# A distance-weighted attention in a twelve-part decoder kernel: one written order for all engines, with its grid computed inside the attention ahead of it

## The reference, cut to what matters

```python
scores = jnp.einsum('bhid,bhjd->bhij', qh, kh) / jnp.sqrt(jnp.float32(DH))
s_ = jnp.where(maskb, scores, -1e+32)
p = jax.nn.softmax(s_, axis=-1) * maskb.astype(scores.dtype)
cum = jnp.cumsum(p, axis=-1)
tot = jnp.sum(p, axis=-1, keepdims=True)
pos = jnp.abs(idx[None, :] - idx[:, None]).astype(scores.dtype)[None, None]
dist_scores = jnp.sqrt(jnp.clip((tot - cum) * pos, 0.0, None))
gamma = -jax.nn.softplus(gammas)[None]
diff = jnp.exp(jax.nn.sigmoid(pdiff))[:, None]
total_effect = jnp.clip(jnp.exp(dist_scores * gamma * diff), 1e-05, 100000.0)
scores = scores * total_effect
scores = jnp.where(maskb, scores, -1e+32)
scores = jax.nn.softmax(scores, axis=-1)
scores = scores.at[:, :, 0, :].set(0.0)
return jnp.einsum('bhij,bhjd->bhid', scores, vh)
```

## Time and profile before

| | us |
|---|---|
| median of 3 runs | 1520.55 (1520.49 to 1525.33) |
| the profiled execution | 1524.32 |
| its span | 1522.5 |
| DVE busy in it | 1058.7 (70%) |
| PE busy | 923.5 (61%) |
| ACT busy | 600.3 (39%) |
| POOL busy | 116.3 (8%) |

### The profile page before, as it was taken

How to read it: one execution, slowest core, us unless ns; L and a number is a source line. 1 busy time by engine, 2 the same in 40 slices (tenths; PEclk the granted TensorE clock), 3 DMA queues, 4 the chain that set the end, 5 groups by cost and what they waited for, 6 DMA issues and landing times. The chain is left out here.

```text
span 1522.5 us, 18302 instructions
## 1 busy us (share of the span) xinstructions
PE 923.5 (61%) x6195; PEld 610.9 (40%) x6195; DVE 1058.7 (70%) x2437; ACT 600.3 (39%) x1197; POOL 116.3 (8%) x249
## 2 busy tenths in 40 slices
PE   4844243445885204437979636999685405876877
PEld 2522132222553103337855413666453203543654
DVE  4868989975563799882348675999396584976843
ACT  2634555541442404442116426554064100553632
POOL 0110000101000000000110120000101001011110
PEclk9975667677897556768989857999598656998978
DMA  5000000001233400001000000000000000000000
GB/s 180 2 1 0 0 0 0 0 0 42 58 86 107 207 0 1 1 0 49 1 1 2 1 0 1 1 1 1 1 1 2 0 0 0 1 2 0 2 1 14
DMA packets 25382, 29.17 MB, mean 19 GB/s; under 512 B 657, under 2 KB 22033, under 8 KB 24274
## 3 DMA queue, kind: packets, MB, share of 16 engines
q1 hardware_dynamic: 25298, 28.09, 5.6%
HBM read 18.65 MB, written 9.44 MB: 18 GB/s over the span
## 5 line engine op out<-in xcount | busy, mean ns | idle before, releaser
L1766 DVE TENSOR_TENSOR_SCAN l2a_hs<-l2a_decay,l2a_b_ps 128x512 f32<-128x512 f32 x64 | 78.0, 1221 | 14.3 <-ACT l2a_decay L1696 6.1
L1621 PEld LDWEIGHTS l2a_b_ps<-l2a_diag,l2a_uT 128*128 128x128 f32 x512 | 64.1, 191 | 39.2 <-issue 37.9
L2152 PE MATMUL l1w_mem_ps<-l1a_rows,l1w_post 128*128 128x64 f32 x16 | 4.3, 363 | 110.6 <-DVE l1a_rows L2292 110.6
L1621 PE MATMUL l2a_b_ps<-l2a_diag,l2a_uT 128*128 128x128 f32 x512 | 69.9, 280 | 1.9 <-DVE l2a_hs L1766 1.7
L1629 PE MATMUL l2a_acc_ps<-l2a_hc,pack 128*128 128x512 f32 x128 | 65.5, 595 | 1.0 <-DVE l2a_hc L1777 1.0
L2265 DVE MATCH_REPLACE8 l1w_minus<-l1w_low,l1w_minus 128x129 f32<-128x129 f32 (+39 forms) x264 | 64.4, 256 | 0.0
L2259 DVE MAX8 l1w_low<-l1w_minus 128x8 f32<-128x129 f32 (+37 forms) x332 | 59.5, 254 | 0.4
L777 PE MATMUL l0x_scores<-pack,l0x_prob 128*128 128x128 f32 x128 | 25.4, 363 | 53.2 <-ACT l0x_prob L912 53.2
L1696 ACT ACTIVATE l2a_decay<-l2a_dt,pack 128x1016 f32<-128x1016 f32 x32 | 36.4, 1141 | 45.4 <-DVE l2a_hs L1766 45.4
L2180 ACT ACTIVATE l1w_score<-l1w_mix_ps 128x264 f32<-128x264 f32 (+7 forms) x29 | 11.4, 447 | 107.3 <-DVE l1a_rows L2292 92.2
L2159 PE MATMUL l1w_at_ps<-l1w_post,l1a_rows 128*128 128x128 f32 x256 | 43.1, 344 | 13.4 <-ACT l1a_rows L2203 13.4
(11 more groups left out here) (592 smaller groups left out, 2749.9 us busy)
## 6 DMA issues: line engine op xcount, KB each, us to landing
scores_dram<-l1p_dots SPq DMA_DIRECT2D x8, 1056.0 KB, 6.3
l1a_rows<-scores_dram SPq DMA_DIRECT2D x8, 1056.0 KB, 13.0
pack<-in_pack SPq DMA_DIRECT2D x1, 697.5 KB, 9.5
pack<-in_pack SPq DMA_DIRECT2D x2, 321.5 KB, 6.7
pack<-in_pack SPq DMA_DIRECT2D x1, 612.0 KB, 11.5
pack<-in_pack SPq DMA_DIRECT2D x1, 576.0 KB, 10.5
pack<-in_pack SPq DMA_DIRECT2D x1, 514.0 KB, 8.1
x_tok<-in_x SPq DMA_DIRECT2D x1, 512.0 KB, 4.3
```

The lines of the kernel that those rows point to most:

```text
L1621: mm = nc.tensor.matmul(bx_ps(n)[:, j * S:(j + 1) * S], uT[:, c, b, :], diag[:, s % 2, b, :], start=True, stop=True)
L1766: nc.vector.tensor_tensor_scan(hs[:, n % 2, :], decay[:, k % 2, batches, :].rearrange("p b t -> p (b t)"), bx_ps(n), 0.0, ALU.mult, ALU.ad ...
```

## The change

The grid and the head rates become an object, `Distances`, whose steps are put into the ACT and DVE programs of `attention` when it runs for `l0a`. `distance_attention` is rewritten: no options, no hardware loop, one order written out over `now` from 0 to 9; q, km and v have two buffers, and the transposes have a PSUM bank of their own. The rates are squared, so that rate, inverse sum and grid go under one square root: for every head one DVE instruction multiplies the remaining mass by the head's scalar and by the grid (`dist`). The root therefore gives the exponent at once, and ACT takes it with scale -1. The second softmax subtracts its maximum as the bias of ACT's exponential, one instruction for each head. The first maximum of a half is one reduction.

```diff
@@ attention
+              distances=None):
...
+                if distances:
+                    distances.act_begin(act)
                 for now in range(-1, B + 2):
...
                     if inside(now):
                         copy_sums(now)
+                    if distances:
+                        distances.act_step(act, now)
...
                 cm.need(dve, name)
+                if distances:
+                    distances.dve_begin(dve)
...
                         maximum(now + 1, 1)
                         prefix_difference(now + 1)
+                    if distances:
+                        distances.dve_step(dve, now)
@@
+class Distances:
...
+    def act_begin(self, act):
+        act.wait_ge(self.size_set, 1)
+        self.nc.scalar.activation(self.growth[:], self.growth[:], ACT.Exp, scale=-1.0).then_inc(self.decay_set, 1)
+        act.wait_ge(self.decay_set, 1)
+        self.nc.scalar.activation(self.growth[:], self.growth[:], ACT.Ln, bias=1.0).then_inc(self.growth_set, 1)
+        act.wait_ge(self.cm.pdiff_loaded, 16)
+
+    def act_step(self, act, now):
+        if 0 <= now < B:
+            self.nc.scalar.activation(self.spread[:, now, :], self.cm.pdiff[:, now, :], ACT.Exp,
+                                      scale=-1.0).then_inc(self.minus_exp, 1)
+        if 0 <= now - 1 < B:
+            act.wait_ge(self.inverse_set, now)
+            self.nc.scalar.activation(self.grid[:, now - 1, :], self.grid[:, now - 1, :], ACT.Exp,
+                                      scale=2.0).then_inc(self.twice_exp, 1)
...
+    def dve_step(self, dve, now):
...
+        if 0 <= now < B:
+            dve.wait_ge(self.minus_exp, now + 1)
+            nc.vector.tensor_scalar(self.spread[:, now, :], self.spread[:, now, :], 1.0, None,
+                                    ALU.add).then_inc(self.spread_set, 1)
+            dve.wait_ge(self.spread_set, now + 1)
+            nc.vector.reciprocal(self.grid[:, now, :], self.spread[:, now, :]).then_inc(self.inverse_set, 1)
+        if 0 <= now - 2 < B:
+            dve.wait_ge(self.twice_exp, now - 1)
+            nc.vector.tensor_tensor(self.grid[:, now - 2, :], self.grid[:, now - 2, :], self.cm.col("apart"),
+                                    ALU.mult).then_inc(self.grid_set, 1)
@@ distance_attention, PE
                 def score(b, half):
                     pe.wait_ge(qk_set, b + 1)
+                    after(pe, scaled_set, 2 * (b - 1) + half + 1)
...
+                for now in range(B + 2):
+                    if inside(now - 1):
+                        transpose_probs(now - 1, 0, 0)
+                    if inside(now - 2):
+                        project_out(now - 2)
+                    if inside(now):
+                        project_v(now)
+                    if inside(now - 1):
+                        transpose_probs(now - 1, 0, 1)
+                        weigh(now - 1, 0)
+                        transpose_probs(now - 1, 1, 0)
+                        transpose_probs(now - 1, 1, 1)
+                        weigh(now - 1, 1)
+                        transpose_sums(now - 1)
+                    if inside(now - 2):
+                        transpose_norm(now - 2)
+                    if inside(now + 1):
+                        score(now + 1, 0)
+                        score(now + 1, 1)
+                    if inside(now + 2):
+                        project_qk(now + 2)
+                    if inside(now - 1):
+                        transpose_out(now - 1)
@@ ACT
+                def exponential(b, half):
+                    act.wait_ge(shift_set, 2 * b + half + 1)
+                    after(act, turn_mm, turn(b - 1, half, 1) + 1)
+                    for h in range(HALF):
+                        last = nc.scalar.activation(prob[:, half, h, :], dist[:, half, h, :], ACT.Exp,
+                                                    bias=last_mx[:, half, h:h + 1], scale=scale)
+                    last.then_inc(prob_set, 1)
...
+                for now in range(B + 2):
+                    if inside(now - 1):
+                        exponential(now - 1, 1)
+                    if inside(now):
+                        first_weights(now, 0)
+                    if inside(now - 1):
+                        copy_probT(now - 1, 0, 0)
+                    if inside(now - 2):
+                        copy_out(now - 2)
+                    if inside(now):
+                        first_weights(now, 1)
+                        copy_v(now)
+                    if inside(now - 1):
+                        copy_probT(now - 1, 0, 1)
+                        copy_probT(now - 1, 1, 0)
+                        copy_probT(now - 1, 1, 1)
+                    if inside(now):
+                        root(now, 0)
+                    if inside(now - 1):
+                        copy_sums(now - 1)
+                    if inside(now):
+                        root(now, 1)
+                        effect(now, 0)
+                        effect(now, 1)
+                    if inside(now - 2):
+                        ln.act_copy(act, nc, cm, nT_ps, now - 2)
+                    if inside(now):
+                        exponential(now, 0)
@@ DVE
+                dve.wait_ge(distances.grid_set, B)
...
+                def remaining(b):
...
+                    nc.vector.tensor_tensor(every(rate), every(rate), gamma2[:], ALU.mult).then_inc(rate_set, 1)
+                    dve.wait_ge(rate_set, 3 * b + 3)
+                    for half in range(2):
+                        after(dve, prob_set, 2 * (b - 1) + half + 1)
+                        for h in range(HALF):
+                            last = nc.vector.scalar_tensor_tensor(
+                                out=dist[:, half, h, :], in0=left[:, half, h, 1:W], scalar=rate[:, half, h:h + 1],
+                                in1=grid[:, b, :], op0=ALU.mult, op1=ALU.mult)
+                        last.then_inc(product_set, 1)
...
+                copy_qk(0)
+                constants()
+                for now in range(B + 2):
+                    if inside(now):
+                        for half in range(2):
+                            differences(now, half)
+                        remaining(now)
+                    if inside(now - 2):
+                        statistics(now - 2)
+                    if inside(now + 1):
+                        copy_qk(now + 1)
+                    if inside(now - 2):
+                        ln.dve_scale(dve, nc, cm, now - 2)
+                    if inside(now - 1):
+                        divide(now - 1)
+                    if inside(now):
+                        second_scores(now)
```

612 lines of the change are left out of this document (174 added, 438 removed).

## The result

| | before | after |
|---|---|---|
| first comparison, median | 1522.84 us (1519.40 to 1525.33, 7 runs) | 1512.54 us (1506.69 to 1515.18, 7 runs) |
| second comparison, median | 1524.78 us (11 runs) | 1510.22 us (1505.83 to 1513.17, 6 runs) |
| the profiled execution, its span | 1524.32, 1522.5 | 1511.67, 1509.4 |
| `l0a` ends at | 95.25 | 110.93 |
| gap to the first maxima of `l0x` | 18.60 | 7.06 |

The ratio is 0.9933 (95% interval 0.9913 to 0.9953) in the first comparison and 0.9904 (0.9877 to 0.9931) in the second. Both attentions together give 14.7 us, where the forecast was 19.9.

The account below looks back on a forecast made before the run. DVE was taken to bound the long `l0x` stretch and be nearly full in `l0a`. Terms 16.9 - 11.6 - 30.0 + 4.8 = -19.9 took 1520.55 to 1500.6 us, range 1490 to 1512.

Parts of the forecast that it names:

- Part 1, the gap: Between `l0a` and the first maxima of `l0x`: 7.0 us instead of 18.60, -11.6, as whole-grid passes on DVE go.
- Part 2, `l0a`: Grid steps moved into `l0a`: DVE work plus a 1.15 us stall, batch 7.63 to 9.90, +16.9 in all.
- Rival (a): Moved steps cost only their work, or the products cost 0.20: -29, 1491.5 us; chance 0.10.
- Rival (d): PE's clock stays at 1.2 GHz in both attentions: up to 1535 us, slower; chance 0.06.
- Part 3, `l0x`: Batches of `l0x` fall to 23.3 us through fewer DVE passes and score waits; loop 188.0 against 217.97, -30.0.
- four copies from one bank in turn with PE, 1.4 us each (0.60 after 0.81 idle): ACT's copies in an `l0x` batch, expected to end at about 11.1 us, with a table load until 12.4.
- the margin of 0.2: In an `l0x` batch, ACT's table load ends at 12.4 us and the product comes at 12.6.
- 1.2 for copies that hold the first root back now and then: Allowance of 1.2 us over the `l0x` loop, added to eight batches of 23.3 us.
- rival (b): ACT's queue is late in `l0x`, first weights or root late, 5 to 9 us: 1508; chance 0.09.
- rival (e): No change, 1521.8: `l0a` pays +22 and the written order holds DVE 2 us more a batch in `l0x`; chance 0.06.
- Rival (c), the table load: In `l0x`, a table load delays ACT's next activation by as much again, 8 x 1.28 = 10: 1510.8; chance 0.02.
- Part 4, the tail: After the last second scores of `l0x`: small exponentials, and copies alternating with PE (another 2.4), +4.8 us.

Follow-up runs that it names:

- e3: Changed kernel with all of exp(-pdiff) as one pass at the head of ACT's program in `l0a`: 1504.25 us, ratio 0.9868.
- e1: Kernel before, with only the grid and head rates made in steps inside `l0a`, old distance attention kept: 1536.12 us against 1524.77, ratio 1.0081.
- e2: Changed kernel with the move undone, the grid made in whole passes before the batches of `l0x`: 1506.43 us, ratio 0.9889.
- e5: Changed kernel with PE's transposes of the second half put ahead of the first half's weighing in `l0x`: 1505.86 us, ratio 0.9885.
- e4: Changed kernel with filler mask matmuls into an unused half bank in PE's waits of `l0x`: 1502.85 us, ratio 0.9854.
- e6: Changed kernel with the last exponentials as before, one pass a half behind a subtraction on DVE: 1525.33 us, ratio 1.0006.
- e10: Changed kernel with grid steps put in DVE's idle time in `l0a` and e5's order of PE, no filler: 1483.59 us, ratio 0.9745.
- e8: Changed kernel with grid steps in DVE's idle time in `l0a`, e5's order of PE and e4's filler: 1483.38 us, ratio 0.9754.
- e11: The same program as e8, run once more: 1486.50 us, ratio 0.9747.

## Why the prediction was right and wrong

**Part 1, the gap: right.** 7.06 for 7.0. The first scores ran at clock 0.50, as assumed.

**Part 2, `l0a`: the mechanism right, the sum partly by luck.** +15.7 for +16.9. The stall was forecast at 1.15 and is 0.94, the reciprocal is 0.95, the period 9.66 for 9.90. But two errors cancel. Up to the last difference of batch 7 (82.67 before, 92.19 after) the steps cost 9.5 us, where the forecast has 12.4 for these six; the last two and the end cost 6.2, for 3.5 and the 1.0 for a falling clock. There the last addition waits 5.54 us, and batch 6's statistics stand behind it. The last division then comes 4.2 us after the begin of ACT's copy of the sums (103.00), in e3 1.35 after it, so this wait was not in idle time. And the clock did fall at the end, to 0.50, while in the kernel before it was 1.00 until 94.1. The stretch at the end of `l0a` and the last division:

```profile
97.00:110.93 13.93, 6.26 (x47) 4.01 (x47) 5.03 (x18) 3.22 (x9) 2.76 (x8) 0.50 0.00 1
```

```profile
107.19 0.25 DVE L605 RECIPROCAL l0a_rz<-l0a_sums_ps 128x16 f32<-128x16 f32 x1
```

That the move alone loses (5.3 forecast) is shown by e1 (6.7) and e2 (4.9), and that the wait is misplaced by e3. Rival (a), that only the work counts, falls with the stall. Rival (d), which needed a slow clock in both attentions, had it in `l0x` but in `l0a` at the end only.

**Part 3, `l0x`: wrong, and here is the step that failed.** The loop gave 26.3, not 30.0. The products were right (16 in 4.29 us, 0.27 each), the small exponentials too (16 in 4.78), and DVE's waits for scores went from 18.1 us to 2.2. The failing step is "four copies from one bank in turn with PE, 1.4 us each (0.60 after 0.81 idle)". That row stands in `l0a`, at clock 1.00, and I used it for a stretch at 0.64, a mean of 1.00 and 0.50. At 0.50 a turn takes 1.87 us (0.60 + 1.27), and 2.91 (0.60 + 2.31) where the weighing lies between. From the end of the exponentials to the end of the last copy it was to be 11.1 - 3.5 = 7.6 us; it is 177.73 - 168.22 = 9.5. The 1.9 more ate the margin of 0.2, pushed the second root 1.1 past its product, and made the batch 24.20. e5 takes the weighing out from between the copies and lands on 23.16; e4 raises the clock and lands on 23.48. So the term that was mis-sized is "1.2 for copies that hold the first root back now and then": it measured 5.9 (191.67 against 185.73 in e5). The rest of that sum, 186.8, was 1.1 too high, which hid a part of the miss. One of the prediction's own signs of being wrong is there, that the copies hold back the first root in every batch. What came true was rival (b) with its condition ("at PE's half clock it is gone, 0.5 to 1.1 a batch is lost"), to which I gave 0.09. The chance was too low by the rows on hand: the clock in that very stretch was already 0.64. Of rival (e), the late root behind the copies came true at about half its price of 2 us a batch, and the +22 in `l0a` did not.

The Trainium skill, page "TensorE: Matmul & The Clock Gate", section "HAM oscillation — how this bites in real kernels", says that repeated waits can leave each burst cold. The traces agree in part. In `l0x` the clock was 0.50, with pieces of 1 us and waits of 0.7 to 3.2 between them, but it was 0.50 in 8.2 us of PE work without a wait as well. In the kernel before PE waited 15.68 us, began again at 165.60, and the clock was 0.50 until 169.2 and then 1.00, so only the begin of that burst was cold:

```profile
165.60 1.97 PE L777 MATMUL l0x_scores<-pack,l0x_prob 128*128 128x128 f32 x8 [15.68 <-ACT l0x_prob L912]
```

In `l0a`, where PE is idle for 10.3 of 38.38 us, the clock was 1.00 and the rule did not bite.

**Rival (c), the table load: wrong.** The load before the effects, now on the path, starts at 181.54 and the first effect at 182.84; the one before the roots starts at 177.74 and the root at 179.04. So a switch costs 1.30 also on the path. The 2.66 us of the Trainium skill, page "ScalarE: Activation LUTs", section "What ACT_TABLE_LOAD costs", are not seen here either.

**Part 4, the tail: direction right, size wrong.** +7.4 for +4.8. The first term, 2.4 for the small exponentials, is what e6 measured (2.4). The second, 2.4 for copies that alternate with PE, measured 5.1, as the turns are again at the half clock. The four copies of the last step:

```profile
313.05 0.57 ACT L873 ACTIVATE l0x_probT<-l0x_turn_ps 128x512 f32<-128x512 f32 x1
...
315.61 0.60 ACT L873 ACTIVATE l0x_probT<-l0x_turn_ps 128x512 f32<-128x512 f32 x1 [1.74 <-PE l0x_turn_ps L776]
318.52 0.60 ACT L873 ACTIVATE l0x_probT<-l0x_turn_ps 128x512 f32<-128x512 f32 x1 [2.31 <-PE l0x_turn_ps L776]
320.39 0.60 ACT L873 ACTIVATE l0x_probT<-l0x_turn_ps 128x512 f32<-128x512 f32 x1 [1.27 <-PE l0x_turn_ps L776]
```

They are 1.9 to 2.9 us apart. With the clock at 0.83 (e4) the tail is 17.77, close to the forecast 17.4.

**The sum.** Against the forecast the attentions lack 5.2 us: loop +3.7, tail +2.6, `l0a` -1.2, gap +0.1. The loop's part is settled by e4 and e5, the tail's by e4 and e6. The rest of the miss, 1512.54 against 1500.6, is not in the attentions as profiled: the reference point of 1520.55 was 2.3 us low (1522.84 in the same comparison), and the 1180 us behind the attentions vary by 6 us between two executions of one kernel. The second comparison, 14.6 us between medians, is near the 14.7 of the profile.

**What stays open.** Why the clock stayed at 0.50 in `l0x` although PE's busy share rose; and why one execution of a program is granted the full clock for longer than the next. No run told either.

## What to carry to other kernels

A duration that contains another engine's turn holds only at that engine's clock: take it from a stretch with the same granted clock, or price it at both levels, above all where the margin is a few tenths. Work moved beside other work costs its place in the queue as much as its time: the same grid cost 15.7 us of `l0a` batch by batch and nothing that shows in waits that the timeline already had. And order a serving engine's queue so that what the next engine waits for goes first; moving one call behind two others gave 1.04 us a batch in the middle of the loop.

## What the runs showed of the hardware that was not expected

- The granted clock does not follow the busy share of PE: 0.64 at 86.47 of 217.97 us, 0.50 at 114.94 of 191.67, 0.71 at 124.90 of 187.70, and 1.00 in `l0a` at 28.06 of 38.38. Part of the higher share at 0.50 is the slower clock itself. A clock between the levels is a mean of both: 0.64 was 10 us at 1.00 and 17 at 0.50 in each batch from the third on.
- Useless matmuls made the kernel faster (e4), but a better order made them superfluous (e10 against e8 and e11).
- Two executions of one kernel agree within 0.02 us over the 192 us of `l0x`, while the whole varies by 6 us, nearly all of it in `l3x`, at a mean clock of 0.84 and 0.91. A stretch of the trace tells a difference of 1 us that the medians do not, where its clock is the same in both.
